# Second graph layer: the sums along edges as three long scans over features laid out end to end, instead of 33 short scans per chunk

## The chip, the cores and the metric

One Trainium2 chip, one of its cores. The metric is the device time of one execution in microseconds (us), the median of the runs. The engines are PE (TensorE), DVE (VectorE), ACT (ScalarE), POOL (GpSimd) and SP (SyncE, which here only issues transfers).

## The reference

Two graph layers on 12,500 nodes with 32 features, over 200,000 edges sorted by target node, each followed by a residual and a layer norm. The change touches only the second layer:

```python
s_src = h @ attn_w[:d]
s_dst = h @ attn_w[d:]
e = s_src[src] + s_dst[dst]
e = jnp.where(e >= 0, e, LEAKY_SLOPE * e)
m = jax.ops.segment_max(e, dst, num_segments=N)
ex = jnp.exp(e - m[dst])
denom = jax.ops.segment_sum(ex, dst, num_segments=N)
alpha = ex / denom[dst]
out = jax.ops.segment_sum(h[src] * alpha[:, None], dst, num_segments=N)
```

So for every node there is a maximum over its edges, a sum of exponentials, and a weighted sum of 32 features of the source nodes.

## The kernel before

The program is a row of blocks, with all engines meeting between two of them: index preparation, the first layer, its layer norm, the second layer's edges (4480 to 6750 us of the span, in round numbers), and the second layer's end (`y1_d` read back by node, layer norm, output).

In the second layer's edge block, partition p of 125 holds 1600 consecutive edges. They are worked in 40 chunks of C = 40 edges per partition; two chunks, h = 0 and h = 1, make one turn of a hardware loop of 20 turns, and each tile that is double-buffered has an h in its name.

- **POOL** gathers the source rows (32 features and `s_src`, in `tab_d`): 40 indirect transfers per chunk, one for each edge column, 128 rows each (L1152). Before a chunk it waits for the chunk's indices, `idxb`.
- **DVE** (function `chunk`, L1180 to L1209) adds the two scores (`lk`, L1187), applies the slope (`ee`), runs a scan for the maximum so far (`mx`, L1189), and prepares `ex`. ACT takes the exponential (L1159). DVE makes the decay `dec` (L1195; 0 where a new node begins, since `kp` is 0 there) and the weighted features `wx` (L1196). Then 33 scans along the chunk's 40 edges, one for each of 32 features (L1205) and one for the sum of exponentials (L1202): z[c] = dec[c] * z[c-1] + wx[c], each with the last value of the chunk before as its start. Most steps have a semaphore wait on DVE's own earlier step (`step`, L1178).
- **ACT** also copies the maximum into `Z` (L1160).
- **SP** issues, for each chunk, the store of `Z` into `y1_d` (L1129), and behind it the loads for the chunk after the next: indices (`idxb`, L1118), then `sdr` and `kpb` (L1123, L1124). The store waits for the chunk's last scan (`d_z`), and the index load stands behind the store in the same queue. So POOL can start chunk n+2 only after the scans of chunk n.

Of the kernel before, what the change touches and what calls it, by code (L numbers as in the profile page):

```python
# [5 lines left out]
def gnn_resnorm_kernel(nc, x, src, dst, emb, vec, weight, W1, W2, attn, out):  # L6
# [3 lines left out]
    ALU = mybir.AluOpType  # L10
# [3 lines left out]
    N, DIM = x.shape  # L14
    E = src.shape[0]
    NEMB, HID = W1.shape
    P = 125
# [37 lines left out]
    with ctx:  # L55
# [68 lines left out]
        with ExitStack() as st:  # L124
            def sbt(name, shape, dt=f32):
                return st.enter_context(nc.sbuf_tensor(name, shape, dt))
# [961 lines left out]
        with ExitStack() as st:  # L1088
# [17 lines left out]
            dec = sbt("dec", [P, C])  # L1106
            wx = sbt("wx", [P, C * DIM])
            Z = two("Zb", C * R1)

            with nc.Block() as block:  # L1110
                @block.sync
                def _(sp):
                    def load(ch, h, t):
# [5 lines left out]
                        sp.wait_ge(S(f"d_z{h}"), t)  # L1119
                        sp.sem_inc(S("go_sp"), 1)  # L1120
                        sp.wait_ge(S(f"d_st{h}"), t * 16)
                        sp.sem_inc(S("go_sp"), 1)
# [3 lines left out]
                    def store(ch, h, t):  # L1126
                        sp.wait_ge(S(f"d_z{h}"), t + 1)
                        sp.wait_ge(S(f"d_zm{h}"), t + 1)
                        sp.dma_start(y1_d[0:E, :].rearrange("(p c) f -> p (c f)", c=EP)[:, bass.ds(ch * C * R1, C * R1)], Z[h][:, :]).then_inc(S(f"d_st{h}"), 16)  # L1129
# [25 lines left out]
                @block.scalar  # L1155
                def _(act):
                    def chunk(h, t):
                        act.wait_ge(S("d_pre"), t * 2 + h + 1)
                        nc.scalar.activation(ex[:, :], ex[:, :], ACT.Exp).then_inc(S("d_exp"), 1)  # L1159
                        nc.scalar.activation(Z[h][:, :].rearrange("p (c f) -> p c f", f=R1)[:, :, DIM + 1],  # L1160
                                             mx[h][:, 1:C + 1], ACT.Copy).then_inc(S(f"d_zm{h}"), 1)

                    with act.Fori(0, PAIRS) as t:
                        for h in range(2):
                            chunk(h, t)

                @block.vector
                def _(dve):
# [3 lines left out]
                    def chunk(h, t):  # L1172
                        n = [0]

                        def step(ins):
# [18 lines left out]
                        dve.wait_ge(S("d_exp"), t * 2 + h + 1)  # L1194
                        V.scalar_tensor_tensor(dec[:, :], ex[:, C:2 * C], 1.0, kp[h][:, :], ALU.min, ALU.mult)  # L1195
                        step(V.tensor_tensor(wx[:, :].rearrange("p (c f) -> p c f", f=DIM), g[:, :, 0:DIM],  # L1196
                                             ex[:, 0:C].rearrange("p (c f) -> p c f", f=1).broadcast_to([P, C, DIM]), ALU.mult))
                        V.memset(one[:, :], 0.0).then_inc(S(f"d_wx{h}"), 1)
                        assert n[0] == STEPS
                        zv = Z[h][:, :].rearrange("p (c f) -> p c f", f=R1)  # L1200
                        zp = Z[1 - h][:, :].rearrange("p (c f) -> p c f", f=R1)
                        V.tensor_tensor_scan(out=zv[:, :, DIM], data0=dec[:, :], data1=ex[:, 0:C], initial=zp[:, C - 1, DIM:DIM + 1],  # L1202
                                             op0=ALU.mult, op1=ALU.add)
                        for f in range(DIM):
                            last = V.tensor_tensor_scan(out=zv[:, :, f], data0=dec[:, :],  # L1205
                                                        data1=wx[:, :].rearrange("p (c f) -> p c f", f=DIM)[:, :, f],
                                                        initial=zp[:, C - 1, f:f + 1], op0=ALU.mult, op1=ALU.add)
# [7 lines left out]
                    dve.wait_ge(S("d_init"), 3)  # L1215
# [3 lines left out]
                    dve.wait_ge(S("d_zm1"), PAIRS)  # L1219
                    V.tensor_copy(tail1[:, :], Z[1][:, (C - 1) * R1:C * R1]).then_inc(S("d_tail"), 1)  # L1220
                    dve.wait_ge(S("d_tail"), 1)
# [121 lines left out]
```

## Time and profile before

| | |
|---|---|
| median of 3 runs | 6929.51 us (6928.4 to 6939.59) |
| the profiled execution | 6937.29 us, span 6935.5 us |
| POOL busy | 4829.8 us, 70% of the span |
| DVE busy | 3611.6 us, 52% |
| PE busy | 3336.5 us, 48% (first layer only) |
| ACT busy | 2498.8 us, 36% |
| second layer's gathers (L1152) | 1600, first start 4482.69, last start 6723.86 us |

A group of the profile reads: line, engine, operation, output and inputs, count, busy time and mean duration of one, and then the idle time of the engine just before them with what ended it. "issue" is idle time that no recorded event explains, and "remote" a wait on a semaphore whose setter the record does not give.

### The profile page before, as it was taken

How to read it: one execution, taken by the hardware profiler on the slowest of the kernel's cores; microseconds unless marked ns; L12 is line 12 of the kernel's file. 1: busy time of each engine (PE TensorE's matmuls, PEld its weight loads, DVE VectorE, ACT ScalarE, POOL GpSimd, SP SyncE). 2: the span in 40 equal slices, each digit the busy share in tenths (PEclk: the TensorE clock that was granted, in tenths of full speed). 3: DMA queues.
4: the chain of work that ended last, by engine and by line, in shares of the span. 5: the costliest groups of instructions: out<-in, count | busy, mean ns of one | idle time of the engine just before them, and what ended most of it. 6: DMA issues, size and time to landing. Idle time of an engine off the chain costs nothing. (4 is left out here: it accounts for less than half of the span.)

```text
span 6935.5 us, 56399 instructions
## 1 busy us (share of the span) xinstructions
PE 3336.5 (48%) x12859; PEld 1619.6 (23%) x12859; DVE 3611.6 (52%) x5473; ACT 2498.8 (36%) x3555; POOL 4829.8 (70%) x4416
## 2 busy tenths in 40 slices
PE   0005999999999999999999980000000000000000
PEld 0003444444444444444444430000000000000000
DVE  4225888788887888888888862012222222212221
ACT  0005666666666666666666650000000000000000
POOL 4576777777777777777777628777666676677657
PEclk9999999999999999999999995555555555555555
DMA  3411111111111111111111101111111111111111
GB/s 138 160 39 36 30 28 30 30 29 30 30 30 30 30 28 27 31 31 29 30 31 30 23 13 11 12 21 25 26 27 21 29 25 24 24 25 25 24 26 20
DMA packets 275726, 228.08 MB, mean 33 GB/s; under 512 B 194512, under 2 KB 251465, under 8 KB 273006
## 3 DMA queue, kind: packets, MB, share of 16 engines
q0 software_dynamic: 131424, 79.08, 8.3%
q1 hardware_dynamic: 144082, 147.06, 6.6%
q14 instruction: 203, 1.66, 0.1%
q8 instruction: 17, 0.28, 0.0%
HBM read 137.03 MB, written 88.30 MB: 32 GB/s over the span
## 5 line engine op out<-in xcount | busy, mean ns | idle before, releaser
L1152 POOL DMA_INDIRECT gxb<-tab_d,idxb x1600 | 1537.3, 961 | 707.6 <-issue 626.2
L535 POOL DMA_INDIRECT gx<-in_x,idx x1540 | 1679.0, 1090 | 411.1 <-issue 368.4
L862 DVE TENSOR_TENSOR prod<-G_ps,hid 128x1000 f32<-128x1000 f32 x1200 | 1420.8, 1193 | 618.6 <-PE G_ps L738 303.9
L752 PE MATMUL R_ps<-sums,red 128*48 128x500 f32 x2400 | 1297.2, 624 | 0.0
L1244 PE MATMUL R_ps<-dm,ones 125*125 125x125 f32 x2 | 0.8, 494 | 2598.0 <-DVE dm L1273 2598.0
L631 ACT ACTIVATE FT<-T_ps 128x500 fp32r<-128x500 f32 x1200 | 707.0, 589 | 524.5 <-PE T_ps L721 323.0
L721 PE MATMUL T_ps<-ident,HL 125*128 125x125 f32 x4800 | 753.5, 280 | 270.1 <-ACT HL L625 189.5
L542 POOL TENSOR_TENSOR sums<-prod 128x500 f32<-128x500 f32 x400 | 502.7, 1257 | 516.3 <-DVE prod L862 312.4
L1159 ACT ACTIVATE ex<-ex 125x80 f32<-125x80 f32 x40 | 10.8, 269 | 2214.8 <-issue 1117.7
L1205 DVE TENSOR_TENSOR_SCAN Zb<-dec,Zb,wx 125x40 f32<-125x40 f32 x1280 | 333.3, 294 | 722.3 <-issue 721.3
L721 PEld LDWEIGHTS T_ps<-ident,HL 125*128 125x128 f32 x4800 | 574.1, 143 | 484.8 <-ACT HL L625 189.8
L619 ACT ACTIVATE HL<-F 125x768 fp32r<-125x768 f32 x400 | 654.7, 1637 | 7.5 <-POOL F L548 7.5
L1244 PEld LDWEIGHTS R_ps<-dm,ones 125*125 125x125 f32 x2 | 0.5, 307 | 2598.1 <-DVE dm L1273 2598.1
L637 ACT ACTIVATE hid<-H_ps 128x500 f32<-128x500 f32 x800 | 473.3, 592 | 319.6 <-PE H_ps L728 267.8
L738 PE MATMUL G_ps<-FT,wst 128*128 128x500 f32 x1600 | 585.9, 448 | 0.0
L869 DVE TENSOR_TENSOR sums<-prod 128x1000 f32<-128x1000 f32 x400 | 536.1, 1340 | 6.9
L728 PE MATMUL H_ps<-FT,wh 128*128 128x500 f32 x800 | 404.4, 506 | 90.1 <-ACT hid L637 83.4
L738 PEld LDWEIGHTS G_ps<-FT,wst 128*128 128x128 f32 x1600 | 244.0, 192 | 666.4 <-issue 380.8
L741 PE MATMUL G_ps<-FT,wst 128*128 128x500 f32 x800 | 353.4, 442 | 64.6 <-DVE prod L862 64.6
L849 DVE TENSOR_TENSOR HL<-F,HL 125x768 fp32r<-125x768 f32 x200 | 341.7, 1708 | 43.5 <-ACT HL L619 42.2
L1187 DVE TENSOR_TENSOR lk<-sdf,gxb 125x40 f32<-125x40 f32 x40 | 9.6, 241 | 635.1 <-DMA gxb<-tab_d,idxb 542.9
L742 PE MATMUL G_ps<-FT,wst 128*128 128x500 f32 x800 | 320.6, 401 | 0.0
(190 smaller groups left out, 4268.7 us busy)
## 6 DMA issues: line engine op xcount, KB each, us to landing
y_d<-Zb SPq DMA_DIRECT2D x40, 664.1 KB
gx<-in_x,idx POOLq DMA_INDIRECT x1600
gxb<-tab_d,idxb POOLq DMA_INDIRECT x1600
xd_d<-zeros SPq DMA_DIRECT2D x16, 1562.5 KB
xv<-xd_d SPq DMA_DIRECT2D x40, 625.0 KB
y_d<-zr SPq DMA_DIRECT2D x40, 625.0 KB
em<-in_edge_attr SPq DMA_DIRECT2D x40, 195.3 KB
kp<-keep_d SPq DMA_DIRECT2D x40, 156.2 KB
```

Of the source, the lines that this page charges most:

```text
L535: nc.gpsimd.indirect_dma_start(out=gx[h][:, c * DIM:(c + 1) * DIM], out_offset=None, in_=x, in_offset=bass.IndirectOffsetOnAxis(idx[h][:, ...
L542: nc.gpsimd.tensor_tensor(sums2[k][:, 0:GW], prod[0][:, 0:GW], prod[0][:, GW:2 * GW], ALU.add).then_inc(S("b_addp"), 1)
L619: A.activation(HLp[(h * SP + q) % 2][:, :, :, r, 0, :], Fv[h][:, q * PCW:(q + 1) * PCW].rearrange("p c (t f) -> p c t f", f=KF), ACT.Copy) ...
L631: A.activation(FT[k][:, i * GW:(i + 1) * GW], T_ps[:, 0:GW], ACT.Copy).then_inc(S("b_FT"), 1)
L637: A.activation(hid[k][:, i * GW:(i + 1) * GW], H_ps[:, 0:GW], ACT.Relu, scale=HSCALE).then_inc(S("b_hid"), 1)
L721: last = Tn.transpose(T_ps[:, c * P:(c + 1) * P], HL[g // PCG % 2][:, col0:col0 + 128].bitcast(f32), ident[0:P, 0:P])
L728: Tn.matmul(H_ps[:, 0:GW], wh[:, i * 128:(i + 1) * 128], FT[k][:, 2 * GW:3 * GW], start=True, stop=True).then_inc(S("b_H"), 1)
L738: last = Tn.matmul(q[:, g0:g0 + GW], wst[:, w0:w0 + 128], FT[k][:, i * GW:(i + 1) * GW], start=True, stop=True)
L752: last = Tn.matmul(R_ps[0:NOUT, 0:GW], red[:, i * NOUT:(i + 1) * NOUT], sums2[k][:, i * GW:(i + 1) * GW], start=(i == 0), stop=(i == 2))
L862: V.tensor_tensor(prod[i][:, :].rearrange("p (a e) -> p a e", a=2), gv, hid[k][:, :].rearrange("p (a e) -> p a e", a=2), ALU.mult).then_in ...
L869: V.tensor_tensor(sums2[k][:, GW:3 * GW].rearrange("p (i e) -> p i e", i=2), q[:, :, 0], q[:, :, 1], ALU.add).then_inc(S("b_add"), 1)
L1152: nc.gpsimd.indirect_dma_start(out=gx[h][:, c * T1:(c + 1) * T1], out_offset=None, in_=tab_d, in_offset=bass.IndirectOffsetOnAxis(idx[h][: ...
```

## The change

`wx`, `dec` and `Z` get the layout feature after feature: 33 rows (32 features and the sum of exponentials) of C1 = 41 columns, end to end. Column 0 of each row carries the last value of the chunk before (in `wx`) and a 0 (in `dec`), so that a scan can run over the border of two rows. Three scans of 11 rows each (451 elements) replace the 33. New are one DVE copy for the carry column, a wider `dec` (11 times 40 elements, the same for all three scans), a second exponential on ACT, and an ACT copy that turns 33 x 40 results back into the order of `y1_d`, in a new tile `zr`, which SP stores. The store waits for this copy. In the SP queue the loads of `sdr` and `kpb` no longer wait for the scans and the store two chunks before.

```diff
@@ second layer, tiles @@
-            dec = sbt("dec", [P, C])
-            wx = sbt("wx", [P, C * DIM])
-            Z = two("Zb", C * R1)
+            C1 = C + 1
+            FS = T1 // 3
+            dec = sbt("dec", [P, FS * C1])
+            wx = sbt("wx", [P, T1 * C1])
+            Z = two("Zb", T1 * C1)
+            zr = two("zrb", C * R1)
@@ SP @@
                         sp.dma_start(idx[h][0:P, :], ...).then_inc(S(f"d_idx{h}"), 16)
-                        sp.wait_ge(S(f"d_z{h}"), t)
-                        sp.sem_inc(S("go_sp"), 1)
-                        sp.wait_ge(S(f"d_st{h}"), t * 16)
-                        sp.sem_inc(S("go_sp"), 1)
                     def store(ch, h, t):
-                        sp.wait_ge(S(f"d_z{h}"), t + 1)
-                        sp.wait_ge(S(f"d_zm{h}"), t + 1)
-                        sp.dma_start(y1_d..., Z[h][:, :]).then_inc(S(f"d_st{h}"), 16)
+                        sp.wait_ge(S(f"d_zr{h}"), t * 2 + 2)
+                        sp.dma_start(y1_d..., zr[h][:, :]).then_inc(S(f"d_st{h}"), 16)
@@ ACT @@
-                        nc.scalar.activation(ex[:, :], ex[:, :], ACT.Exp).then_inc(S("d_exp"), 1)
-                        nc.scalar.activation(Z[h]...[:, :, DIM + 1], mx[h][:, 1:C + 1], ACT.Copy).then_inc(S(f"d_zm{h}"), 1)
+                        nc.scalar.activation(wx[:, DIM * C1 + 1:T1 * C1], ex[:, 0:C], ACT.Exp).then_inc(S("d_exp"), 1)
+                        nc.scalar.activation(ex[:, C:2 * C], ex[:, C:2 * C], ACT.Exp).then_inc(S("d_exp"), 1)
+                        act.wait_ge(S(f"d_st{h}"), t * 16)
+                        act.sem_inc(S("go_act"), 1)
+                        zo = zr[h][:, :].rearrange("p (c f) -> p c f", f=R1)
+                        nc.scalar.activation(zo[:, :, DIM + 1], mx[h][:, 1:C1], ACT.Copy).then_inc(S(f"d_zr{h}"), 1)
+                        act.wait_ge(S(f"d_z{h}"), t + 1)
+                        nc.scalar.activation(zo[:, :, 0:T1], Zv[h][:, 1:], ACT.Copy).then_inc(S(f"d_zr{h}"), 1)
@@ DVE @@
-                        dve.wait_ge(S("d_exp"), t * 2 + h + 1)
-                        V.scalar_tensor_tensor(dec[:, :], ex[:, C:2 * C], 1.0, kp[h][:, :], ALU.min, ALU.mult)
+                        V.tensor_copy(wxv[:, 0, :], Zv[1 - h][:, C, :])
+                        dve.wait_ge(S("d_exp"), t * 4 + h * 2 + 2)
+                        V.scalar_tensor_tensor(dec...[:, :, 1:], rows(ex[:, C:2 * C]), 1.0, rows(kp[h][:, :]), ALU.min, ALU.mult)
-                        V.tensor_tensor_scan(out=zv[:, :, DIM], data0=dec[:, :], data1=ex[:, 0:C], initial=zp[:, C - 1, DIM:DIM + 1], ...)
-                        for f in range(DIM):
-                            last = V.tensor_tensor_scan(out=zv[:, :, f], data0=dec[:, :], data1=wx...[:, :, f],
-                                                        initial=zp[:, C - 1, f:f + 1], ...)
+                        dve.wait_ge(S(f"d_zr{h}"), t * 2)
+                        dve.sem_inc(S("go_dve"), 1)
+                        for i in range(3):
+                            part = slice(i * FS * C1, (i + 1) * FS * C1)
+                            last = V.tensor_tensor_scan(out=Z[h][:, part], data0=dec[:, :], data1=wx[:, part], initial=0.0, ...)
                         last.then_inc(S(f"d_z{h}"), 1)
```

On DVE, in the first chunk of a turn, from the last step before the exponential to the end of the chunk. Before (`one_d` is a one-element memset that carries a semaphore, REGISTER_ALU computes a wait's value; SCALAR_TENSOR_TENSOR is also the name under which a scan stands here):

```order
L1193 MEMSET one_d 125x1
L1194 REGISTER_ALU
L1195 SCALAR_TENSOR_TENSOR dec<-ex,kpb 125x40
L1196 TENSOR_TENSOR wx<-gxb,ex 125x1280
L1178 REGISTER_ALU
L1198 MEMSET one_d 125x1
L1202 SCALAR_TENSOR_TENSOR Zb<-dec,Zb,ex 125x40
L1205 SCALAR_TENSOR_TENSOR Zb<-dec,Zb,wx 125x40 x32
L1209 REGISTER_ALU
```

The same place in the changed kernel:

```order
L1198 MEMSET one_d 125x1
L1199 COPY wx<-Zb 125x33
L1200 ISA
L1202 SCALAR_TENSOR_TENSOR dec<-ex,kpb 125x11x40
L1204 TENSOR_TENSOR wx<-gxb,wx 125x40x32
L1183 REGISTER_ALU
L1206 MEMSET one_d 125x1
L1212 SCALAR_TENSOR_TENSOR Zb<-dec,wx 125x451 x3
L1214 REGISTER_ALU
```

The 33 scans have become three, one copy is new, and the rest of the chunk keeps its place. On SP, the queue between two stores of the loop, as a piece of the difference:

```order
-L1129 ISA [waits d_zm0,d_z0]
-L1129 DMA y_d<-Zb 125x1360
-L1114 ISA
-L1118 ISA [waits d_gx0,d_wx0]
-L1118 DMA idxb<-in_src 125x40
-L1123 DMA sdr<-sd_d 125x40 [waits d_z0,d_st0]
...
+L1129 ISA [waits d_zr0]
+L1129 DMA y_d<-zrb 125x1360
+L1119 ISA
+L1123 ISA [waits d_gx0,d_wx0]
+L1123 DMA idxb<-in_src 125x40
+L1124 DMA sdr<-sd_d 125x40
```

The order of the transfers is the same, and the index load still stands behind the chunk's store; the store now waits for ACT's copy (`d_zr`), and the `sdr` load for nothing of its own.

## Rows read from the trace of the kernel before

**Rows 1.** The page: busy time of each engine; DVE's busy tenths in 40 slices.

```profile
PE 3336.5 (48%) x12859; PEld 1619.6 (23%) x12859; DVE 3611.6 (52%) x5473; ACT 2498.8 (36%) x3555; POOL 4829.8 (70%) x4416
...
DVE  4225888788887888888888862012222222212221
```

**Rows 2.** The page, three of the costliest groups.

```profile
L1152 POOL DMA_INDIRECT gxb<-tab_d,idxb x1600 | 1537.3, 961 | 707.6 <-issue 626.2
L535 POOL DMA_INDIRECT gx<-in_x,idx x1540 | 1679.0, 1090 | 411.1 <-issue 368.4
...
L1205 DVE TENSOR_TENSOR_SCAN Zb<-dec,Zb,wx 125x40 f32<-125x40 f32 x1280 | 333.3, 294 | 722.3 <-issue 721.3
```

**Rows 3.** Line L1118 (index load): who waited for it (us, times).

```profile
  POOL gxb L1152: 226.1, 20
```

**Rows 4.** Timeline at the second layer's start: start, duration, instruction, idle before.

```profile
4482.69 1.00 POOL L1152 DMA_INDIRECT gxb<-tab_d,idxb  x1 [2.79 <-DMA idxb<-in_src]
```

**Rows 5.** Groups of instructions by line, 5220 to 5250 us.

```profile
L1152 POOL DMA_INDIRECT gxb<-tab_d,idxb x24 | 22.7, 945 | 7.3 <-issue 7.3
L1205 DVE TENSOR_TENSOR_SCAN Zb<-dec,Zb,wx 125x40 f32<-125x40 f32 x16 | 4.9, 308 | 16.8 <-issue 16.8
```

**Rows 6.** Groups of instructions by line, 5170 to 5208 us.

```profile
L1152 POOL DMA_INDIRECT gxb<-tab_d,idxb x31 | 29.3, 945 | 9.4 <-issue 9.4
```

**Rows 7.** Timeline of all engines around one pause of POOL, 5030 to 5105 us.

```profile
5033.43 0.94 POOL L1152 DMA_INDIRECT gxb<-tab_d,idxb  x1 [0.30 <-issue]
...
5035.92 0.26 DVE L1187 TENSOR_TENSOR lk<-sdf,gxb 125x40 f32<-125x40 f32 x1 [10.68 <-DMA gxb<-tab_d,idxb]
...
5041.60 0.30 DVE L1202 TENSOR_TENSOR_SCAN Zb<-dec,Zb,ex 125x40 f32<-125x40 f32 x1 [1.55 <-issue]
...
5083.78 0.95 POOL L1152 DMA_INDIRECT gxb<-tab_d,idxb  x1 [0.30 <-issue]
5087.25 0.29 SPq L1129 DMA_DIRECT2D y_d<-Zb  x1
5087.57 0.18 DVE L1182 TENSOR_SCALAR rst<-kpb 125x40 f32<-125x40 f32 x1 [10.01 <-remote]
...
5094.74 0.70 SPq L1118 DMA_DIRECT2D idxb<-in_src  x1
5095.25 0.94 POOL L1152 DMA_INDIRECT gxb<-tab_d,idxb  x1 [10.52 <-issue]
...
5101.52 1.51 DVE L1196 TENSOR_TENSOR wx<-gxb,ex 125x1280 f32<-125x1280 f32 x1
...
5104.60 0.30 DVE L1202 TENSOR_TENSOR_SCAN Zb<-dec,Zb,ex 125x40 f32<-125x40 f32 x1 [1.57 <-issue]
```

**Rows 8.** Timeline, the next pause's end and the scans behind it.

```profile
5144.29 0.95 POOL L1152 DMA_INDIRECT gxb<-tab_d,idxb  x1 [0.30 <-issue]
...
5158.23 2.06 POOL L1152 DMA_INDIRECT gxb<-tab_d,idxb  x1 [12.99 <-DMA idxb<-in_src]
...
5159.73 6.40 DVE L1205 TENSOR_TENSOR_SCAN Zb<-dec,Zb,wx 125x40 f32<-125x40 f32 x32
```

**Rows 9.** Timeline of DVE in the chunk after that, 5210 to 5220 us.

```profile
5210.82 0.23 DVE L1187 TENSOR_TENSOR lk<-sdf,gxb 125x40 f32<-125x40 f32 x1 [43.73 <-DMA gxb<-tab_d,idxb]
...
5214.29 2.64 DVE L1205 TENSOR_TENSOR_SCAN Zb<-dec,Zb,wx 125x40 f32<-125x40 f32 x13
5217.32 0.30 DVE L1205 TENSOR_TENSOR_SCAN Zb<-dec,Zb,wx 125x40 f32<-125x40 f32 x1 [0.38 <-issue]
```

**Rows 10.** Groups by line and shape, all of the span.

```profile
L835 DVE TENSOR_TENSOR_SCAN F<-kp,xt 125x328 f32<-125x328 f32 x160 | 125.5, 825 | 11.9 <-ACT xt L591 11.9
...
L597 ACT ACTIVATE zr<-Z 125x1280 f32<-125x1280 f32 x40 | 101.7, 2542 | 7.0 <-DMA y_d<-zr 7.0
```

**Rows 11.** Timeline at the second layer's end, 6720 to 6755 us.

```profile
6723.86 0.95 POOL L1152 DMA_INDIRECT gxb<-tab_d,idxb  x1 [0.30 <-issue]
...
6739.81 6.36 DVE L1205 TENSOR_TENSOR_SCAN Zb<-dec,Zb,wx 125x40 f32<-125x40 f32 x32
...
6754.50 1.21 POOL L1252 DMA_INDIRECT fixr<-y_d,fix_i  x1 [29.70 <-POOLq L1110]
```

More of the change, by code:

```diff
@@ L1105, in gnn_resnorm_kernel @@
             ex = sbt("ex", [P, 2 * C])
-            dec = sbt("dec", [P, C])
-            wx = sbt("wx", [P, C * DIM])
-            Z = two("Zb", C * R1)
+            C1 = C + 1
[4 more added lines that the diff above has]
+            zr = two("zrb", C * R1)
+            wxv = wx[:, :].rearrange("p (f c) -> p c f", c=C1)
+            Zv = [z[:, :].rearrange("p (f c) -> p c f", c=C1) for z in Z]
             with nc.Block() as block:
@@ L1126, in store @@
                     def store(ch, h, t):
-                        sp.wait_ge(S(f"d_z{h}"), t + 1)
-                        sp.wait_ge(S(f"d_zm{h}"), t + 1)
-                        sp.dma_start(y1_d[0:E, :].rearrange("(p c) f -> p (c f)", c=EP)[:, bass.ds(ch * C * R1, C * R1)], Z[h][:, :]).then_inc(S(f"d_st{h}"), 16)
+                        sp.wait_ge(S(f"d_zr{h}"), t * 2 + 2)
+                        sp.dma_start(y1_d[0:E, :].rearrange("(p c) f -> p (c f)", c=EP)[:, bass.ds(ch * C * R1, C * R1)], zr[h][:, :]).then_inc(S(f"d_st{h}"), 16)
                     sp.wait_ge(S("d_idxz"), 2)
@@ new lines, in chunk @@
+                        dve.wait_ge(S("d_exp"), t * 4 + h * 2 + 2)
+                        rows = lambda a: a.rearrange("p (f c) -> p f c", f=1).broadcast_to([P, FS, C])
+                        V.scalar_tensor_tensor(dec[:, :].rearrange("p (f c) -> p f c", c=C1)[:, :, 1:], rows(ex[:, C:2 * C]), 1.0,
+                                               rows(kp[h][:, :]), ALU.min, ALU.mult)
+                        step(V.tensor_tensor(wxv[:, 1:, 0:DIM], g[:, :, 0:DIM],
+                                             wx[:, DIM * C1 + 1:T1 * C1].rearrange("p (c f) -> p c f", f=1).broadcast_to([P, C, DIM]), ALU.mult))
@@ L1198, in chunk @@
                         V.memset(one[:, :], 0.0).then_inc(S(f"d_wx{h}"), 1)
                         assert n[0] == STEPS
[L1200 to L1203, printed above, removed]
-                        for f in range(DIM):
-                            last = V.tensor_tensor_scan(out=zv[:, :, f], data0=dec[:, :],
-                                                        data1=wx[:, :].rearrange("p (c f) -> p c f", f=DIM)[:, :, f],
-                                                        initial=zp[:, C - 1, f:f + 1], op0=ALU.mult, op1=ALU.add)
+                        dve.wait_ge(S(f"d_zr{h}"), t * 2)
@@ L1208, in chunk @@
+                        dve.sem_inc(S("go_dve"), 1)
+                        for i in range(3):
+                            part = slice(i * FS * C1, (i + 1) * FS * C1)
+                            last = V.tensor_tensor_scan(out=Z[h][:, part], data0=dec[:, :], data1=wx[:, part], initial=0.0, op0=ALU.mult, op1=ALU.add)
                         last.then_inc(S(f"d_z{h}"), 1)
@@ L1214, in _ @@
                     V.memset(Z[1][:, :], 0.0).then_inc(S("d_init"), 1)
-                    dve.wait_ge(S("d_init"), 3)
+                    V.memset(dec[:, :], 0.0).then_inc(S("d_init"), 1)
+                    dve.wait_ge(S("d_init"), 4)
                     with dve.Fori(0, PAIRS) as t:
@@ L1218, in _ @@
                             chunk(h, t)
-                    dve.wait_ge(S("d_zm1"), PAIRS)
-                    V.tensor_copy(tail1[:, :], Z[1][:, (C - 1) * R1:C * R1]).then_inc(S("d_tail"), 1)
-                    dve.wait_ge(S("d_tail"), 1)
+                    V.tensor_copy(tail1[:, 0:T1], Zv[1][:, C, :]).then_inc(S("d_tail"), 1)
+                    V.tensor_copy(tail1[:, T1:R1], mx[1][:, C:C1]).then_inc(S("d_tail"), 1)
+                    dve.wait_ge(S("d_tail"), 2)
         with ExitStack() as st:
```

4 lines of the change are left out of this document (removed).

## The prediction

> **What bounds the kernel now.** I read the page first. No engine is busy through the whole span [rows 1], so each stage has its own limit. In the second layer's edges it is POOL: 1600 gathers of 961 ns, with 707.6 us of idle time between them [rows 2]. A gather is followed by 0.30 us that belongs to it (24 gathers with 7.3 us, 31 with 9.4 us [rows 5, 6]); 1600 times 0.30 is some 484 us. The rest, about 220 us, must be real pauses, and the wait on the index load names them: POOL waited 20 times, 226.1 us in all [rows 3]. One of the 20 stands before the first gather (2.79 us [rows 4]). The other 19 hold 223.3 us, less 19 ordinary gaps of 0.30 us: **217.6 us in which POOL stands still between chunks**.
>
> The timeline shows why. A chunk of gathers takes about 50.3 us. One ends at 5034.4, DVE starts on it at 5035.92, its first sum scan is at 5041.60, and the last is complete only at about 5087.4, when SP's store and DVE's next chunk both start. 7.5 us later SP issues the index load, and POOL resumes at 5095.25 after 10.52 us of pause [rows 7]. From the end of gathering one chunk to the start of the chunk after the next that is 60.9 us, while the gathers in between cover 50.
>
> The reader is to see that the scans are slow in one state and not in another. Between 5160 and 5166, 32 of them take 6.40 us, 0.20 us each [rows 8]. In the state that begins near 5217 [rows 9], each is still recorded at about 0.30 us but they start about 1.4 us apart (16 of them cover 21.7 us [rows 5]): 45.8 us for 33 [rows 7]. I call it the slow-issue state. SP is in it too, with 7.5 us from a store to the next index load. It costs per instruction and not per element: the 1280 elements of `wx` took 1.51 us inside it [rows 7]. It follows POOL: it begins some 59 us after POOL resumes from the pause of 12.99 us, and is over by 5159.7, when POOL had been still for the 13 us before [rows 8, 9]. The gathers themselves are not slower in it, 945 ns and 0.30 us on both sides [rows 5, 6]. What it is, no row tells.
>
> **The change, part by part.**
>
> *Removed: 33 short scans, added: 3 long ones.* The trace has no scan of 451 elements. The nearest is 328 elements at 825 ns [rows 10] against 40 at 294 ns [rows 2], 1.84 ns per further element; that gives 825 + 123 x 1.84 = 1.05 us. By plain proportion to the 328 it is 1.13 us, which I take as the upper end. Three are 3.2 us, or 4.2 us if the slow-issue state starts them 1.4 us apart. So the scans of a chunk fall from 45.8 us to about 4, and from 6.6 to 3.2 outside that state.
>
> *Added on the way from scans to index load.* The carry copy (one instruction: 0.2 to 1.4 us), a second exponential (0.3 to 1.4), a wider `dec` (440 elements; between 0.2 us, the 40-element steps, and the 1.5 us of `wx`'s 1280), and ACT's turning copy of 1320 elements, for which the first layer has a twin of 1280 at 2.54 us [rows 10]; so 2.6 us, and 4 with one slow issue. Together 4 to 8 us. The two `sem_inc` waits taken out of SP's queue stand behind the index load, so they give this path nothing.
>
> *The path again.* Landing and preparation 7.2 us (5034.4 to 5041.6), additions 8, scans 4.2, SP 7.5, landing 0.5: about 27 us. With the longest preparation shown, 17.0 us from 5087.57 to 5104.60 [rows 7], and its landing wait, about 39 us. Both are under the 50 us that the gathers of the other chunk cover. **All 19 pauses go: -217.6 us.** The spare of 11 to 23 us is what hides the additions; it holds even if the slow-issue state never ends, which I expect, since the long pauses that ended it are gone. ACT waits for the scans and for an old store, but behind it only the next chunk's exponential is queued, some 50 us away.
>
> *The rate of the gathers.* This sets the time from now on. 961 ns against 945 undisturbed [rows 2, 5] is 25 us over 1600, from DVE and ACT working beside it; the first gather after a long pause even took 2.06 us [rows 8]. Best case: all 25 us vanish. Worst case of the ordinary kind: the first layer's gathers took 1090 ns [rows 2] beside a DVE that is busy for 80% or more [rows 1]. Here it would be busy for about 7 us of 50 (scans 3.2, `wx` 1.5, the small steps), a sixth of that load, so 145/6 = 24 ns over 945, or 969: +13 us. I take 0, in between.
>
> *The end.* From the last gather's end (6724.8) to POOL's next work is 29.7 us [rows 11]. Scans there run fast and shrink from 6.6 to 3.2 us, DVE no longer has the chunk before in front of it (scans could begin at about +7 instead of +15), and 2.6 us of ACT plus the copies come in before the store. 29.7 - 8 - 3.4 + 4 = 22.3: **-7 us**, 0 to -11.
>
> **Sum.** 6937.3 - 217.6 - 7 + 0 = 6712.7 us for a profiled execution. The one profiled before was 7.8 us over its median; I take off half of that, since three runs don't say which is usual: **6709 us**.
>
> **A rule weighed against the trace.** Rows first: outside the slow-issue state a short scan costs 0.20 us from start to start, and inside it 1.4. The Trainium skill, VectorE: DVE Perf Modes, section "The TRN2 errata", says that a DVE instruction on SBUF data pays a fixed latency once (58 cycles at 0.96 GHz in its table), so that many small tiles cost more than one large. By that rule 33 scans cost a few us more than three, which POOL's 50 us cover anyway, and the time would not move. The trace agrees outside the state, and contradicts it inside, where it is the issue that costs.
>
> **The rivals.**
>
> - *No change* (6 in 100). The waiting is not the scans' number. Either the slow-issue state charges by scanned element, 1.4 us for 40, so that 451 cost 15.8 us and three of them 47; or SP and the preparation alone fill the 50 us. For: the scans are the only place where the state shows in quantity. Against: `wx`, and SP's 7.5 us without any element. Only the end could gain; 6925 to 6940 us. It decides from about 10 us for one long scan: there the pauses return.
> - *Pauses in part* (7 in 100). A permanent slow-issue state gets deeper, with instructions 2.8 us apart: the 39 us path becomes some 60, as before, in some chunks. Half of the pauses left: 6820 us.
> - *Slower* (5 in 100): **the slow-issue state reaches POOL.** Its steps are multiples of 0.7 us. Without pauses it never ends, and if a gather then starts every 1.40 us (two steps) and not every 1.25, 1600 of them cost 240 us more: 6709 + 240 = 6949 us. It decides from 1.39 us per gather. For: the state follows POOL's own activity. Against: the gathers kept 945 + 300 ns through every slow stretch I read.
> - *More gain* (4 in 100): with a third of the instructions the state goes away, DVE's and ACT's disturbance of the gathers with it: 6685 us.
>
> **How the numbers follow.** The forecast has 78 in 100: 6709, from 6690 (no disturbance of the gathers, whole end gain, the full 7.8) to 6728 (13 us of disturbance, no end gain). To reach 8 in 10 the range takes in the "more gain" case and a wider disturbance: 6684 to 6740. A change under 0.2% (14 us) can't be told from none here. Faster: 78 + 7 + 4 = 89; same 6; slower 5.
>
> **What the profile after would show.** The wait of gathers on the index load: one of about 3 us instead of 20 with 226. L1152's idle time near 485 us, its mean 955 to 970 ns. Last gather near 6506. `Zb` scans 120 times at 1.0 to 1.1 us; the ACT copy at 2.6 us. DVE waiting for gathers in each chunk for 20 us or more. I'm wrong if pauses over 1 us stand between chunks, if a gather starts more than 1.27 us after the last, or if the scans cost several us each.

## The result, and the profile after

The changed kernel takes 6896.8 us (median of 5 runs, 6887.41 to 6899.81) against 6929.51 us (5 runs, 6927.09 to 6939.59). The ratio is 0.9946, with an interval of 0.9931 to 0.996. It is 33 us faster where 220 were forecast, and lies above the range. The profiled execution took 6887.41 us.

The changed kernel's page, the rows that answer to [rows 1, 2]:

```profile
PE 3325.6 (48%) x12859; PEld 1615.5 (23%) x12859; DVE 3452.7 (50%) x4315; ACT 2604.3 (38%) x3635; POOL 4982.4 (72%) x4416
...
L1152 POOL DMA_INDIRECT gxb<-tab_d,idxb x1600 | 1697.9, 1061 | 516.9 <-issue 514.1
L535 POOL DMA_INDIRECT gx<-in_x,idx x1540 | 1669.7, 1084 | 411.3 <-issue 370.8
...
L1192 DVE TENSOR_TENSOR lk<-sdf,gxb 125x40 f32<-125x40 f32 x40 | 9.7, 243 | 1874.7 <-DMA gxb<-tab_d,idxb 1874.7
```

The changed kernel's view of line L1152, its duration (minimum, median, maximum), first and last start, and what ended its waits (us, times):

```profile
L1152 POOL DMA_INDIRECT gxb<-tab_d,idxb x1600: 943/947/2926, 4472.0 to 6683.1; - x178
its engine sat idle before it (us, times) until:
  issue: 514.1, 1599
  DMA idxb<-in_src: 2.8, 1
```

The wait on the index load has shrunk from 226.1 us in 20 times [rows 3] to 2.8 us in one. The pauses are gone. The gathers took their place: idle time fell by 190.7 us (707.6 to 516.9), and their own time rose by 160.6 (1537.3 to 1697.9). The stage from the first gather's start to the last one's end went from 2242.1 us [rows 4, 11] to 2212.0, 30 us less.

The changed kernel's stretches of 112 us in the middle of the stage: length, POOL's busy time, gathers in brackets, the granted clock as a share, DMA share, GB/s:

```profile
5004.84:5116.84 112.00, 85.95 (x80) 0.50 0.15 25
5116.84:5228.84 112.00, 85.94 (x80) 0.50 0.15 25
```

80 gathers fill 112.00 us, then again: **1.400 us each**, where an undisturbed one with its gap took 1.25. The timeline of the changed kernel in one such stretch:

```profile
5008.36 2.46 DVE L1204 TENSOR_TENSOR wx<-gxb,wx 125x1280 f32<-125x1280 f32 x1
5008.60 2.91 POOL L1152 DMA_INDIRECT gxb<-tab_d,idxb  x1 [0.31 <-issue]
...
5010.98 3.08 DVE L1212 TENSOR_TENSOR_SCAN Zb<-dec,wx 125x451 f32<-125x451 f32 x3
5011.81 1.42 POOL L1152 DMA_INDIRECT gxb<-tab_d,idxb  x1 [0.30 <-issue]
...
5014.09 2.56 ACT L1166 ACTIVATE zrb<-Zb 125x1320 f32<-125x1320 f32 x1 [6.13 <-DVE Zb L1212]
...
5016.83 0.29 SPq L1129 DMA_DIRECT2D y_d<-zrb  x1
...
5019.69 0.95 POOL L1152 DMA_INDIRECT gxb<-tab_d,idxb  x1 [0.85 <-issue]
...
5022.31 0.69 SPq L1123 DMA_DIRECT2D idxb<-in_src  x1
...
5025.11 0.69 SPq L1124 DMA_DIRECT2D sdr<-sd_d  x1
...
5048.79 0.95 POOL L1152 DMA_INDIRECT gxb<-tab_d,idxb  x1 [0.30 <-issue]
...
5051.33 1.10 POOL L1152 DMA_INDIRECT gxb<-tab_d,idxb  x1 [0.30 <-issue]
5052.73 1.10 POOL L1152 DMA_INDIRECT gxb<-tab_d,idxb  x1 [0.30 <-issue]
```

Three things make up the longer time: gathers beside `wx` and the scans on DVE (2.91 and 1.42 us for 0.95), single gaps of 0.85 us, and rows of gathers of 1.10 us that start 1.40 us apart. SP needs 5.48 us from store to index load and 2.80 from that to the next load, so the slow-issue state is still there.

The changed kernel's timeline at the end of the stage:

```profile
6683.08 0.95 POOL L1152 DMA_INDIRECT gxb<-tab_d,idxb  x1 [0.30 <-issue]
...
6690.41 3.08 DVE L1212 TENSOR_TENSOR_SCAN Zb<-dec,wx 125x451 f32<-125x451 f32 x3
...
6696.09 0.28 SPq L1129 DMA_DIRECT2D y_d<-zrb  x1
...
6704.38 1.21 POOL L1258 DMA_INDIRECT fixr<-y_d,fix_i  x1 [20.35 <-issue]
```

29.7 us [rows 11] have become 20.4. Of the profiled difference, 49.9 us (6937.3 to 6887.41), 30.1 lie in the stage, 9.3 here, and 10.7 ahead of the stage, which starts at 4472.0 and not at 4482.69 though nothing is changed there. The profile before was 7.8 us over its median and the one after 9.4 under its own; without both, 33 us are left.

### The profile page after: what moved, and what is told of

It is laid out like the page before. It is cut to its first block and busy times, and to the rows that moved or that the text cites. A ratio compares the mean times of both kernels' runs of the same rounds, so it can differ in the third digit from the quotient of the medians.

```text
span 6885.7 us, 55321 instructions
## 1 busy us (share of the span) xinstructions
PE 3325.6 (48%) x12859; PEld 1615.5 (23%) x12859; DVE 3452.7 (50%) x4315; ACT 2604.3 (38%) x3635; POOL 4982.4 (72%) x4416
## 5 line engine op out<-in xcount | busy, mean ns | idle before, releaser
L1152 POOL DMA_INDIRECT gxb<-tab_d,idxb x1600 | 1697.9, 1061 | 516.9 <-issue 514.1
L535 POOL DMA_INDIRECT gx<-in_x,idx x1540 | 1669.7, 1084 | 411.3 <-issue 370.8
L555 POOL TENSOR_TENSOR O<-pb,pg 125x192 f32<-125x192 f32 x200 | 274.9, 1375 | 44.9 <-DVE pb L892 41.8
```

The costliest lines, as they stand in the source:

```text
L535: nc.gpsimd.indirect_dma_start(out=gx[h][:, c * DIM:(c + 1) * DIM], out_offset=None, in_=x, in_offset=bass.IndirectOffsetOnAxis(idx[h][:, ...
L1152: nc.gpsimd.indirect_dma_start(out=gx[h][:, c * T1:(c + 1) * T1], out_offset=None, in_=tab_d, in_offset=bass.IndirectOffsetOnAxis(idx[h][: ...
```

## The experiments

They ran in five comparisons, each with its own runs of the kernel before on the same chip. The kernel before came out at two levels. The reader needs both to read any number below, so they stand first; "stage" is the time from the first gather's start to the last one's end.

| comparison | kernel before, us | kernel | us | ratio [interval] | stage, us |
|---|---|---|---|---|---|
| 1 | 6695.67 | no sums | 6658.94 | 0.9954 [0.9938, 0.9971] | 1997.5 |
| 1 | | index first | 6696.87 | 1.0001 [0.9991, 1.001] | 2026.7 |
| 1 | | half rows | 6721.74 (1 run) | | 2050.2 |
| 1 | | short rows | 6774.81 (1 run) | | 2100.4 |
| 2 | 6926.81 | changed | 6887.58 | 0.9939 [0.9926, 0.9953] | 2211.9 |
| 2 | | wx by rows | 6891.43 | 0.9947 [0.9934, 0.9961] | 2211.8 |
| 2 | | no wx | 6893.45 | 0.9944 [0.9929, 0.9959] | 2211.8 |
| 2 | | no scans | 6888.84 | 0.9945 [0.993, 0.996] | 2212.2 |
| 3 | 6927.3 | half rows | 6889.31 (1 run) | | 2211.9 |
| 3 | | short rows | 6897.88 (1 run) | | 2210.4 |
| 3 | | index first | 6918.08 | 0.9989 [0.9978, 1.0001] | 2230.8 |
| 3 | | no sums | 6888.26 | 0.9942 [0.9925, 0.9958] | 2212.1 |
| 4 | 6931.8 | 36 gathers | 6677.3 (1 run) | | 1989.2 |
| 4 | | spacer | 6970.82 | 1.0053 [1.0036, 1.007] | 2288.4 |
| 4 | | changed | 6897.01 | 0.9951 [0.9938, 0.9965] | 2213.0 |
| 5 | 6689.49 | wide spacer | 7064.87 | 1.0563 [1.0545, 1.058] | 2401.0 |
| 5 | | changed | 6768.65 | 1.012 [1.0103, 1.0137] | 2103.1 |

The same kernel before takes about 6929 us in comparisons 2 to 4, as in the result above, and about 6692 in 1 and 5. I call the first the **capped condition**, the second the **free** one. Times are compared only within one condition.

The two conditions differ in one more thing, which the page shows in its section on DMA issues. The line of the gathers in "no sums", capped, and then in the same kernel, free:

```profile
gxb<-tab_d,idxb POOLq DMA_INDIRECT x1600
gxb<-tab_d,idxb POOLq DMA_INDIRECT x1600, 2.4
```

The last number is the time from issue to landing, and capped traces have none, because most of the landings are not in them. A gather makes 16 semaphore updates as it lands. Each free trace has all 25,600 of them; of as many, the capped traces have 4561 (kernel before), 3173 (changed) and 3141 ("no sums"), and of all landing updates of the program they have 27,763 to 32,104 where the free ones have 62,784, to one. The spacer has the most of the capped ones for the gathers, 6929. So in the capped condition records of events are lost, in the first layer too, where the gathers are no slower for it (1084 ns each, and 1086 in the free "no sums"). Every execution here comes with a recorded span and clock, so none is known to have run without recording.

### Comparison 1 (free condition)

*No sums*: the changed kernel without `dec` and with `wx`, the scans and ACT's turning copy cut to one or two columns, so that DVE and ACT hardly work beside the gathers. Its output leaves the edge sums out.

```diff
-V.scalar_tensor_tensor(dec[:, :]..., rows(ex[:, C:2 * C]), 1.0, rows(kp[h][:, :]), ALU.min, ALU.mult)
-step(V.tensor_tensor(wxv[:, 1:, 0:DIM], g[:, :, 0:DIM], wx...broadcast_to([P, C, DIM]), ALU.mult))
+step(V.tensor_tensor(wxv[:, 1:2, 0:DIM], g[:, 0:1, 0:DIM], wx...broadcast_to([P, 1, DIM]), ALU.mult))
...
-part = slice(i * FS * C1, (i + 1) * FS * C1)
+part = slice(i * FS * C1, i * FS * C1 + 2)
```

> The changed kernel with nearly all of the DVE and ACT work of the edge block left out: no dec, wx for one edge column only, the three scans 2 elements long, the ACT turning copy 66 elements (so the sums are not computed). Theory A, a ceiling: something serves the gathers at 1.40 us each on average and lets POOL run only some 28 us (20 gathers) ahead of it. Then leaving the work out gives nothing: the 1600 gathers take about 2212 us as in the changed kernel (1600 x 1.40 - 28), the median is 6885 to 6900 us, and instead of the few long gathers beside DVE there are more of 1.10 us. Theory B, disturbance: the gathers lose their time to DVE and ACT working beside them (119 us of the 186 us above 0.945 us per gather lie in gathers that overlap such work). Then the gathers fall to about 1.25 to 1.28 us from start to start, the stage to 2000 to 2090 us, and the median to about 6700 to 6790 us.

*Index first*: the kernel before, with its 33 short scans; SP issues the index load ahead of the store.

```diff
 for h in range(2):
+    load_idx(t * 2 + h + 2, h, t + 1)
     store(t * 2 + h, h, t)
```

> The kernel before, with its 33 short scans, but the index load of the chunk after the next is issued ahead of the chunk's store, so that POOL's next chunk no longer waits for the scans (only for wx, which frees the gathered tile). Theory A (ceiling of 1.40 us per gather, 28 us of lead): the pauses of about 10.5 and 13 us shrink or go, and the time falls by at most 28 us and some, to 6895 to 6925 us: the pauses were themselves the result of the ceiling. Theory C, the one of the prediction: the pauses cost 217 us and the slow gathers of the changed kernel come from its own new work; then about 6720 to 6780 us. If DVE, slowed to 1.4 us per instruction, becomes the limit, pauses remain and the time stays near 6930 us.

*Half rows*: the changed kernel, each gather fetches 64 of 128 rows.

```diff
-out=gx[h][:, c * T1:(c + 1) * T1], ... idx[h][:, c:c + 1]
+out=gx[h][0:64, c * T1:(c + 1) * T1], ... idx[h][0:64, c:c + 1]
```

> The changed kernel with gathers of 64 rows instead of 128, as many of them (half of the edges' rows are not gathered and stand as zeros). Theory A1, the ceiling is per row or per descriptor: it becomes 0.70 us per gather, below what POOL needs; the slow-issue state is gone (no gather of 1.10 us, SP issues its loads within 0.5 us of each other), and the gathers start every 1.25 us or less: stage 2010 us or shorter. Theory A2, the ceiling is per gather (one instruction, its 16 engines and its semaphore updates): unchanged at 1.40 us, stage about 2212 us and 6885 to 6900 us in all.

*Short rows*: the changed kernel, a row of 8 numbers (32 bytes) and not of 33.

```diff
+tab8 = tab_d.rearrange("n f -> (n f)")[0:N * 8].rearrange("(n f) -> n f", f=8)
-out=gx[h][:, c * T1:(c + 1) * T1], in_=tab_d
+out=gx[h][:, c * T1:c * T1 + 8], in_=tab8
```

> The changed kernel with gathers of 128 rows of 8 floats (32 bytes) instead of 33 (132 bytes), from a view of the same table (the other features and the score stand as zeros). If the ceiling is in bytes or in the memory's handling of 132-byte rows, it falls away: gathers every 1.25 us, stage about 2010 to 2050 us, median near 6720 us. If it is per row or per gather it stays: stage about 2212 us, 6885 to 6900 us.

Groups on POOL over the whole span, "no sums", then "index first", then "short rows":

```profile
L1152 POOL DMA_INDIRECT gxb<-tab_d,idxb x1600 | 1510.2, 944 | 490.1 <-issue 487.3 <-DMA idxb<-in_src 2.8
```

```profile
L1156 POOL DMA_INDIRECT gxb<-tab_d,idxb x1600 | 1539.4, 962 | 489.9 <-issue 487.3 <-DMA idxb<-in_src 2.7
```

```profile
L1156 POOL DMA_INDIRECT gxb<-tab_d,idxb x1600 | 1613.1, 1008 | 488.3 <-issue 488.3
```

Here 33 short scans a chunk go without any pause. The index load's place can't be the reason, since the kernel before itself is as fast (ratio 1.0001). In this condition the scans have no slow issue. That also means that these four kernels can't say what held the changed kernel in the other condition; they price DVE's disturbance instead. Their expected times, set out for the capped condition, were all missed. With 32-byte rows the gathers are as long as with 132-byte ones in the changed kernel of comparison 5 (1008 and 1010 ns), so bytes don't set their length.

### Comparison 2 (capped condition)

*Changed* is the kernel on record, again. *Wx by rows* writes the same product of `wx` contiguously and reads `g` with a stride. *No wx* computes one column of it, and *no scans* scans 2 elements of 451 three times; each leaves that part of the sums out.

```diff
# wx by rows
-V.tensor_tensor(wxv[:, 1:, 0:DIM], g[:, :, 0:DIM], ...)
+V.tensor_tensor(wx[:, :].rearrange("p (f c) -> p f c", c=C1)[:, 0:DIM, 1:], g[:, :, 0:DIM].rearrange("p c f -> p f c"), ...)
# no wx
+V.tensor_tensor(wxv[:, 1:2, 0:DIM], g[:, 0:1, 0:DIM], ...)
# no scans
+part = slice(i * FS * C1, i * FS * C1 + 2)
```

> The changed kernel itself, beside the kernel before. In the first four experiments the kernel before took 6695.67 us and not 6929.51, and no slow-issue state showed in any trace. If that holds here: no pauses to win, and each chunk's gathers take 52.3 us (as in the first chunks of the changed kernel's trace and in e4_short_rows) against 50.3, so 40 x 2.0 = 80 us more, less some 8 us at the end: the changed kernel is SLOWER than before, near 6768 us, ratio 1.011. Theory A (ceiling): where the state is present (before near 6930), it takes 6885 to 6900. The prediction's own reasoning (gathers hardly disturbed) would give 6690 in both.

> The changed kernel with wx made feature after feature: the product is written in contiguous runs of 40 and the gathered tile is read with a stride of 33, in place of the other way round. Theory: the strided write makes wx 2.46 us instead of 1.48, and a gather that falls on it is stopped for about that long (2.91 and 2.50 us instead of 0.945). If strided reads are cheaper than strided writes, wx returns to 1.5 us and 1 us per chunk comes back: 40 us less than f1_changed where no state is present. If reads with a stride cost the same, no difference. Where the state is present, the ceiling allows no gain at all (6885 to 6900).

> The changed kernel with wx made for one edge column only (a 32-element product; the scans then run over old values), all else kept. It prices wx alone. By the gathers that fall on it (2.91 and 2.50 us, some 1.5 to 2 us above 0.945) it is worth 60 to 75 us of the 112 us between e4_short_rows and e1_no_sums: about 6695 to 6705 us where no state is present. If instead the long scans are what stops the gathers, less than 30 us comes back. Where the state is present: 6885 to 6900 us, since the ceiling holds.

> The changed kernel with its three scans 2 elements long and all else kept (the sums are not computed). It prices the long scans alone: the two gathers after the wx gather took 1.42 and 1.28 us, so 0.8 us per chunk, 32 us in all: about 6735 us where no state is present; 6885 to 6900 us where it is.

Groups on POOL, "changed", then "no wx":

```profile
L1152 POOL DMA_INDIRECT gxb<-tab_d,idxb x1600 | 1697.8, 1061 | 516.9 <-issue 514.1 <-DMA idxb<-in_src 2.9
```

```profile
L1152 POOL DMA_INDIRECT gxb<-tab_d,idxb x1600 | 1679.2, 1049 | 535.3 <-issue 532.6 <-DMA idxb<-in_src 2.7
```

Without `wx` the gathers get 18.6 us shorter in sum and the gaps 18.4 us longer (1697.8 + 516.9 = 2214.7; 1679.2 + 535.3 = 2214.5). The stage is 2211.8 to 2212.2 us in all four. The disturbance by DVE is in the records but not in the end: something else sets 1.40 us per gather, and whatever it doesn't use is filled up with waiting.

### Comparison 3 (capped condition)

The four kernels of comparison 1, word for word.

> e3_half_rows once more (gathers of 64 rows), because the slow-issue state was absent in that comparison (kernel before at 6695.67 us) and present in the second (6926.81 us). Where it is present: if the ceiling of 1.40 us is per row, it becomes 0.70 us per gather and does not bind; then no gather of 1.10 us, loads of SP 0.4 to 1.2 us apart as in e4_short_rows, the gathers' stage near 2050 us and about 6720 us in all, as in e3_half_rows. If it is per gather: stage 2212 us, about 6885 to 6895 us. Where the state is absent: about 6720 us and nothing learned.

> e4_short_rows once more (rows of 32 bytes). Where the state is present: if the ceiling is in bytes it goes away, stage near 2100 us and about 6775 us in all; if it is per row or per gather, stage 2212 us and 6885 to 6895 us. Where absent: about 6775 us.

> e2_idx_first once more (33 short scans, the index load ahead of the store). Where the state is present: DVE's chunk then takes about 62 us at 1.4 us per instruction, more than the 56 us that the ceiling gives per chunk, so DVE becomes the limit by turns and pauses of some us remain; the stage lies between the changed kernel's 2212 and the kernel before's 2242 us, the time between 6890 and 6930. By the prediction's theory (pauses cost their full 217 us) it would be near 6720. Where absent: equal to before, as measured (ratio 1.000).

> e1_no_sums once more (nearly all DVE and ACT work of the sums left out). Where the state is present, theory A gives the same 2212 us for the gathers and about 6875 to 6890 us, all through gathers of 1.10 us now; where absent, 6659 us as measured, with gathers every 1.248 us.

Windows of 112 us of the gathers' line, "no sums" in the capped condition (comparison 3), then the same kernel in the free one (comparison 1):

```profile
5000.00:5112.00 112.00, 84.70 (x81) 0.50 0.15 25
5112.00:5224.00 112.00, 84.70 (x81) 0.50 0.15 25
5224.00:5336.00 112.00, 84.71 (x81) 0.50 0.15 25
```

```profile
5000.00:5112.00 112.00, 84.58 (x91) 0.50 0.17 31
5112.00:5224.00 112.00, 84.71 (x90) 0.50 0.17 29
5224.00:5336.00 112.00, 84.75 (x90) 0.50 0.16 27
```

The window edges cut a gather, hence 81 for 80. One program, the same granted clock, hardly anything beside the gathers, and 80 of them in 112 us there, 90 here. The cap depends neither on DVE's work, nor on rows, nor on bytes: half rows 2211.9 us, short rows 2210.4, no sums 2212.1. Half rows and short rows did leave two things as they were, 32 DMA packets a gather (5120 in 224 us with 160 gathers, in "half rows" and in "no sums") and its 16 landing updates. In "index first" pauses remain beside the 33 scans, though its index load stands ahead of the store in SP's queue.

```profile
L1156 POOL DMA_INDIRECT gxb<-tab_d,idxb x1600 | 1575.0, 984 | 658.4 <-issue 493.9 <-DMA idxb<-in_src 164.5
```

(Groups on POOL of "index first", capped.) 164.5 us of pauses, and its stage still is 1600 times 1.39.

### Comparison 4 (capped condition)

*36 gathers*: the changed kernel with 36 gathers a chunk for 40, 1440 in all; 4 columns of each chunk are not fetched. *Spacer*: a small memset on POOL behind each gather, meant to space the gathers 1.4 us apart so that they never run ahead of the cap, and one wait per chunk.

```diff
# 36 gathers
-for c in range(C):
+for c in range(C - 4):
# spacer (wide spacer: 240 for 32)
+gap = sbt("gap_d", [P, C * 32])
...
+    nc.gpsimd.memset(gap[:, c * 32:(c + 1) * 32], 0.0).then_inc(S("d_gap"), 1)
+pool.wait_ge(S("d_gap"), t * 2 * C + h * C + C)
```

> The changed kernel with 36 gathers per chunk instead of 40 (four edge columns are not gathered and stand as zeros); the rest of the chunk is as it was. If the ceiling is 1.40 us per gather with 28 us of lead, the stage takes 1440 x 1.40 - 28 = 1988 us and the whole some 224 us less than the changed kernel: about 6665 us where the state is present. If the ceiling is a time per chunk (56 us, whatever is in it: the store, the loads), nothing changes: 6888. Where the state is absent: 52.3 - 5.0 = 47.3 us per chunk, 6570 us.

> The changed kernel with a small memset on POOL (32 elements in each of 125 partitions) behind each gather, so that the gathers start further apart of themselves. A memset of this size takes 0.1 to 0.2 us (the 128x16 one in the first stage: 0.109 us), so a gather every 1.4 to 1.5 us. If the slow-issue state is nothing but the lead over a service of 1.40 us per gather, it then does not arise (SP's loads 0.3 to 1.2 us apart, no 1.10 us gathers), and the stage takes 1600 x the new spacing: 2250 to 2400 us, 6925 to 7080 us in all. If the service counts POOL's instructions and not its gathers, the state is there from the first chunk and the stage takes far more, up to 4400 us. Where the state is absent the spacing gives the same 6925 to 7080 us.

> The changed kernel itself once more, for the condition in which it has not been measured. If the kernel before runs near 6695 us (state absent): 6760 to 6775 us, slower by 1.1%, since a chunk's gathers take 52.3 us beside the changed DVE work against 50.3 (e4_short_rows, e2_idx_first). If it runs near 6927: about 6888 again, ratio 0.994.

View of the gathers' line in "36 gathers":

```profile
L1155 POOL DMA_INDIRECT gxb<-tab_d,idxb x1440: 943/947/2950, 4485.1 to 6473.3; - x180
```

4485.1 to 6474.3 is 1989.2 us; 1440 times 1.40 less a head start of 28 us is 1988. So the cap counts gathers, or what each gather makes a fixed number of, such as its packets and landing updates; it is not a time per chunk. The head start is the changed kernel's 1600 x 1.40 - 2212.0 = 28 us, and here it comes out nearly the same (2016 - 1989.2 = 27 us) with a tenth fewer gathers.

The spacer missed. The group of its memsets:

```profile
L1155 POOL MEMSET gap_d<- 125x32 f32 x1600 | 229.6, 144 | 5.4 <-issue 4.8
```

144 ns fit into the 0.30 us that POOL has behind a gather anyway, so next to nothing was spaced. Pauses came back between chunks instead, up to 7.6 us long (the stage grew to 2288.4 us); the new wait at the chunk's end is the likely reason, which no run shows by itself. It excludes one thing only: 1600 more POOL instructions that are no gathers don't count against the cap as gathers do, since twice 1600 at 1.40 would be 4480 us. It also shows something that it was not built for. Counted from the gathers' starts at 1.40 us each, with waiting time not saved up, POOL is never more than 6 us ahead in it. Yet SP needs 4.64 us from store to index load in one chunk (5117.40 to 5122.04 us) and 0.65 in the next (5176.41 to 5177.06).

### Comparison 5 (meant for the capped condition, ran in the free one)

> h2_spacer with a memset of 240 elements in place of 32, since the small one fitted into the 0.30 us between two gathers and left them 1.255 us apart. The 128x256 memset of the first stage took 0.312 us, so some 0.95 + 0.17 + 0.31 + 0.02 = 1.43 to 1.45 us from gather to gather, over the 1.40 us of the service. If the slow-issue state is only the lead over that service, it is gone from the trace (no pauses of 2 to 7 us between chunks, SP's index load within 1 us of the store in every chunk), although POOL now does more; the stage takes 1600 x 1.44 + 40 x 2 (beside DVE's work) = 2390 us, about 7070 us in all. If POOL's memsets count in the service, or the state has another trigger, SP's loads stay 2.8 us apart in most chunks.

> The changed kernel, for the condition without the slow-issue state, if it comes back: 6760 to 6775 us against 6695 (slower by 1.1%). In the other condition 6888 against 6927, as in three comparisons.

The wide spacer's 1.5 us per gather was to show whether SP and DVE issue fast when POOL never gets ahead. In the free condition they do so anyway, so it tells nothing. The changed kernel is the useful one: **slower by 1.2%** than the kernel before on the same chip, as expected for this condition (6760 to 6775 us). View of its gathers' line:

```profile
L1152 POOL DMA_INDIRECT gxb<-tab_d,idxb x1600: 940/944/2940, 4446.7 to 6548.9; - x178
its engine sat idle before it (us, times) until:
  issue: 487.3, 1599
```

The median of 944 ns and the 487.3 us of gaps are those of "no sums"; only single gathers are long. Its timeline in one chunk:

```profile
5025.62 0.94 POOL L1152 DMA_INDIRECT gxb<-tab_d,idxb  x1 [0.30 <-issue]
...
5026.45 2.46 DVE L1204 TENSOR_TENSOR wx<-gxb,wx 125x1280 f32<-125x1280 f32 x1
...
5026.87 2.73 POOL L1152 DMA_INDIRECT gxb<-tab_d,idxb  x1 [0.30 <-issue]
...
5029.07 3.08 DVE L1212 TENSOR_TENSOR_SCAN Zb<-dec,wx 125x451 f32<-125x451 f32 x3
...
5029.90 1.02 POOL L1152 DMA_INDIRECT gxb<-tab_d,idxb  x1 [0.30 <-issue]
5031.23 1.67 POOL L1152 DMA_INDIRECT gxb<-tab_d,idxb  x1 [0.30 <-issue]
...
5034.92 0.29 SPq L1129 DMA_DIRECT2D y_d<-zrb  x1
...
5035.64 0.27 SPq L1123 DMA_DIRECT2D idxb<-in_src  x1
```

Three gathers take 2.73, 1.02 and 1.67 us for 0.94: 2.60 us a chunk, 104 us over 40 chunks, and the stage is 105.6 us longer than that of "no sums" (2103.1 and 1997.5). The short scans with their contiguous `wx` cost 29.2 us by the same measure ("index first", 2026.7). The difference, 76 us, is nearly all of the 79 us by which the change is slower here, if "index first" stands for the kernel before, whose time it has in comparison 1; the free kernel before has no trace of its own. SP goes from store to index load in 0.72 us, where the capped condition needs 5.5 to 7.5.

## Why the prediction was wrong, step by step

**What holds.** The 19 pauses went. A scan of 451 elements takes 1.08 us (1.05 forecast), ACT's copy 2.55 (2.6), the wider `dec` 0.62 (0.2 to 1.5). The end of the stage gained 9.3 us, inside 0 to 11 around 7. The slow-issue state did persist.

**The step that failed: "The rate of the gathers. ... I take 0, in between."** In the capped condition gathers are served every 1.40 us on average. POOL may run some 28 us ahead of that, 20 gathers, and no further. Busy and idle time of the line, less the pauses, were to be 1537.3 + 707.6 - 217.6 = 2027.3 us; they are 2214.8. So the term that I bounded by -25 and +13 us and put at 0 came out as **+187.5 us**, and ate nearly all of the "-217.6". (In the free condition, with hardly anything beside the gathers, it would be 2000.3, which is 1510.2 + 490.1 and near my lower bound.)

**Why the pauses were worth next to nothing.** The kernel before already ran at that rate. Its stage holds 1600 gathers in 2242.1 us [rows 4, 11], which is 1.401 us each, pauses included. I read "945 ns and 0.30 us on both sides" off short stretches [rows 5, 6] and took 1.25 us for POOL's own rate and the rest for a loss. Both were right as records. The pauses were the form in which POOL paid back its lead. Counted from the starts of its gathers against 1.40 us each, the kernel before is never more than 16.7 us ahead; its pair of pauses of 10.5 and 13 us takes that lead back and a little more, so that from the end of one long pause to the next (4932.7 to 5158.2 us) 160 gathers take 225.5 us, 1.409 each. The changed kernel climbs to 27 us ahead within 320 gathers and stays there, and pays in gathers of 1.10 us and gaps of 0.85. At the last gather it is 27.6 us ahead and the kernel before 2.6 us behind: those are the 30 us won in the stage.

The head start shows at the stage's beginning. The changed kernel's windows there:

```profile
4472.00:4500.00 28.00, 21.25 (x23) 0.50 0.12 14
4500.00:4528.00 28.00, 21.60 (x22) 0.50 0.13 13
```

45 gathers in 56 us are 63 us' worth at 1.40: some 7 us ahead. Soon after, SP issues in slow steps, by its queue in the same kernel:

```profile
4533.97 0.29 SPq L1129 DMA_DIRECT2D y_d<-zrb  x1
4541.34 0.70 SPq L1123 DMA_DIRECT2D idxb<-in_src  x1
4543.44 0.70 SPq L1124 DMA_DIRECT2D sdr<-sd_d  x1
4546.25 0.69 SPq L1125 DMA_DIRECT2D kpb<-keep_d  x1
```

So the order that the traces suggest is another than mine: POOL's lead comes first, the slow issue on SP and DVE with it, and the slow issue then stretches 33 short scans until the index load is late. It fits the chunks of the capped condition that I read, the kernel before among them: its slow stretch begins 59 us after a pause (47 gathers, again some 7 us ahead) and is over after the next long one. That the lead causes it was to be tested by the spacers and wasn't, and what the lead fills isn't shown. The lost records come no later: in the changed kernel's trace 143 landing updates are left between 4480 and 4500 us of some 256 that the free "no sums" has in 20 us, 44 in the next 20 us, and 22 to 33 in each 20 us from there on.

**The rival that came true in part.** "The slow-issue state reaches POOL", a gather every 1.40 us, was given 5 in 100 and priced 6709 + 240 = 6949 us. The period is right to three digits. The price is wrong by two terms. The 240 us count from 1.25 us per gather, while the 6709 already held 2027.3 us for the line, 27 more than 1600 times 1.25; and it left out the head start of 28 us. With both, 1600 times 1.40 is 2240, less 28 is 2212, 185 us more than 2027.3, and 6709 + 185 = 6894 us, where 6896.8 was measured. "The gathers kept 945 + 300 ns through every slow stretch I read" was the argument against it. It was true of the kernel before, whose lead never reached the 28 us at which the gathers themselves are held up.

**The disturbance by DVE** was mis-sized too, which shows only in the free condition. I scaled the first layer's 145 ns by DVE's busy share and had 38 us over undisturbed gathers at worst (25 + 13); it is 106 us for the changed kernel, 76 more than for short scans. In the timeline the cost lies in the few gathers beside the long instructions, so their length matters and not only the busy share; `wx` and the scans were not priced apart in the free condition. And `wx` I took at the 1.51 us of before; written with a stride it is 2.46. "Wx by rows", with the stride on the read, has 2435 ns, so the stride costs on either side.

The Trainium skill, SBUF — State Buffer, section "SBUF: two separate sides", says that VectorE and GpSimd share a port pair as an exclusive lock: a VectorE instruction in a two-port mode, or one with two SBUF inputs against a GpSimd one that reads SBUF, keeps the other off it for its whole length. As a case of the two-port kind it names the descriptors of a transfer, which GpSimd writes. `wx` and the scans have two SBUF inputs, and the trace largely agrees: the gathers of 2.73 and 2.91 us end 0.69 us behind the end of `wx` in both conditions, and in comparison 5 each gather that starts inside a scan ends 0.75 us behind that one scan, the one of 1.02 us behind the first (end 5030.17) and the one of 1.67 us behind the third (end 5032.15). It does not agree for gathers of 2.50 us in the capped condition, which start 0.6 us ahead of `wx` and end 0.6 us ahead of its end. The rate of 1.40 us is in no such rule. The Trainium skill, NOTIFIC — the notification-queue block, section 7.1, names queues that can stall an engine when full; no run here shows whether that is it.

**What stays open.** What serves the gathers at 1.40 us, why it does so in the result and in comparisons 2 to 4 and not in 1 and 5, and whether the lead alone brings on the slow issue. DVE's work, rows, bytes and the order in SP's queue are excluded as causes of the cap; the number of gathers counts, or that of their packets or landing updates. The nearest rival was not tested: the recording itself may be what lags, since records are lost in all traces of the capped condition and in none of the free one. Then the cap, the pauses and the 33 us would say nothing of the kernel when it is not recorded. That the first layer loses records without slower gathers speaks for a limit reached only at the second layer's rate, or against this rival; a run without recording, or with fewer semaphore updates per gather, would decide. The free condition is not tied to a chip: comparisons 1 and 2 name the same chip. I have no kernel that beats both in both conditions: in the capped one only fewer gathers helped, and a gather takes one index per partition here, so the work needs all of them.

## What to carry to other kernels

Before you price pauses as a loss, divide the whole stage by its number of repeated instructions: if a round number comes out (1.40 us here, where single ones run at 1.25), the pauses may be how a hidden rate is paid, and taking them away then buys next to nothing. When a small experiment moves the idle time and the busy time of an engine by the same amount in opposite directions, the limit is likely outside of both. Run the kernel before beside each experiment, and look at its absolute time as well as at the ratio: the same change was 0.5% faster and 1.2% slower here, by the level at which the kernel before ran. When one program has two levels, compare also how complete its traces are: a level at which records are missing may belong to the recording.

## What the runs showed of the hardware

- A gather of 128 rows costs 944 ns and a gap of 0.30 us whether a row is 132 or 32 bytes; with 64 rows the timeline has 0.91 us and the same gap.
- In the capped condition the changed kernel's gathers average 1.400 us over 112 us and more, with or without `wx`, scans, half of the rows or most of the bytes, with a head start of about 28 us; SP then issues its loads 2.1 to 2.8 us apart. In the free condition "no sums" has 1.248 us. Whether the cap exists without recording no run shows.
- The capped traces hold 27,763 to 32,104 landing updates of DMAs, the free ones, of the same programs for the most part, 62,784.
- Long DVE instructions stretch single gathers: `wx` of 2.46 us to 2.73 us or 2.91, the long scans to 1.42 or 1.67. Short scans of 282 ns (0.20 us apart) leave a mean of 962 ns.
